# LayerNorm sums moved from GpSimd back to the tensor engine, and a narrower halo, in an eight-core macaron block

## What is computed

```python
x = x + 0.5 * ffn(layernorm(x), w1, b1, w2, b2)
x = x + attn(layernorm(x), ...)
x = x + 0.5 * ffn(layernorm(x), w1, b1, w2, b2)
```

## Time and profile before

| | us |
|---|---|
| median of the two runs shown | 5175.09 (5070.04 and 5280.14) |
| profiled execution | 5069.3 |
| its span, first to last instruction, slowest core (7) | 5067.8 |
| spans of the eight cores | 5056.0 to 5067.8 |
| TensorE matmul busy | 4774.9 (94%) |
| VectorE, ScalarE, GpSimd busy | 512.8, 402.2, 289.6 |
| granted TensorE clock, mean over the span, eight cores | 0.970 to 0.974 |

### The profile page before, as it was taken

One profiled execution on the slowest core, in us unless ns is written; L12 is line 12 of the kernel. 1 busy time (PEld: TensorE's weight loads), 2 busy tenths in 40 slices (PEclk: granted clock), 3 DMA queues, 4 the chain that ended last, 5 costly groups with the idle time before them and its releaser, 6 DMA issues.

```text
span 5067.8 us, 31354 instructions; the slowest of 8 cores (5056.0 to 5067.8 us)
## 1 busy us (share of the span) xinstructions
PE 4774.9 (94%) x11994; PEld 2274.3 (45%) x11994; DVE 512.8 (10%) x721; ACT 402.2 (8%) x628; POOL 289.6 (6%) x360
## 2 busy tenths in 40 slices
PE   5999999999999996999979798599999999999999
PEld 2555555555555552444534333244444444444444
DVE  1010010010010002223223311101000100000000
ACT  1101101101100101111000000100011001100100
POOL 2000000000000001111000000200010010000000
PEclk9999999999999997999989999799999999999999
DMA  4222222222222221333321101022222222222222
GB/s 121 92 85 90 92 87 88 91 87 92 87 89 90 90 89 42 113 105 105 122 87 32 59 27 29 25 75 79 86 72 75 80 89 67 77 85 83 75 84 77
DMA packets 116244, 408.04 MB, mean 81 GB/s; under 512 B 13825, under 2 KB 20097, under 8 KB 116097
## 3 DMA queue, kind: packets, MB, share of 16 engines
q1 hardware_dynamic: 103298, 362.43, 22.5%
q0 software_dynamic: 12800, 43.61, 2.5%
HBM read 379.73 MB, written 26.25 MB: 80 GB/s over the span
## 4 chain that ended last, share of the span: by engine, by line
PE 92%; DVE 2%; DMA 2%; POOLq 1%; issue 1%; ACT 1%; POOL 0%; ACTq 0%; SPq 0%; DVEq 0%
PE ps L150 92%; POOLq L190 1%; DVE pool L165 1%; DMA pool<-gate_sc 1%; ACT pool L160 1%; POOL pool L191 0%; DVE pool L325 0%; DMA pool<-win_cat 0%; DMA X<-T_fm 0%; DVE pool L181 0%; DVE pool L334 0%; DMA pool<-wout_cat 0%; SPq L185 0%; ACTq L54 0%; DVEq L54 0%
## 5 line engine op out<-in xcount | busy, mean ns | idle before, releaser
L150 PE MATMUL ps<-pool 128*128 128x436 f32 (+2 forms) x11792 | 4672.7, 559 | 167.5 <-DVE pool L165 51.5
L150 PEld LDWEIGHTS ps<-pool 128*128 128x128 f32 x11792 | 2249.2, 192 | 2594.3 <-issue 2593.7
L160 ACT ACTIVATE pool<-ps,smalls_s 128x436 f32<-128x436 f32 (+1 forms) x328 | 212.8, 649 | 1782.0 <-PE ps L150 1781.7
L181 DVE SCALAR_TENSOR_TENSOR X<-pool,smalls_s,X 128x436 f32<-128x436 f32 (+1 forms) x72 | 51.0, 708 | 2068.3 <-ACT pool L160 2068.3
L160 ACT ACTIVATE pool<-ps 128x436 f32<-128x436 f32 (+3 forms) x105 | 58.3, 555 | 1776.1 <-PE ps L150 1767.2
L165 DVE TENSOR_TENSOR pool<-pool 1x436 f32<-1x436 f32 (+1 forms) x24 | 17.7, 737 | 1563.2 <-ACT pool L160 1562.7
L160 ACT ACTIVATE pool<-X 128x436 f32<-128x436 f32 (+1 forms) x112 | 65.5, 585 | 895.5 <-DVE X L181 420.1
L150 PE MATMUL ps<-pool,ones_c 128*1 128x436 f32 (+1 forms) x126 | 56.7, 575 | 66.0 <-POOL pool L191 64.4
L185 POOL DMA_DIRECT2D out_fm<-X x32 | 17.3, 542 | 1748.6 <-DVE X L181 1748.6
L150 PE MATMUL ps<-pool,ones_r 1*128 1x436 f32 (+1 forms) x76 | 48.3, 771 | 53.1 <-DVE pool L165 27.3
L191 POOL TENSOR_TENSOR pool<-X 128x436 f32<-128x436 f32 (+1 forms) x14 | 16.0, 1146 | 1418.7 <-DVE X L181 744.9
(11 more groups left out here) (26 smaller groups left out, 272.9 us busy)
## 6 DMA issues: line engine op xcount, KB each, us to landing
pool<-w1r SPq DMA_DIRECT2D x288, 512.0 KB, 3.3
pool<-w2r SPq DMA_DIRECT2D x288, 512.0 KB, 3.3
pool<-in_wr SPq DMA_DIRECT2D x80, 512.0 KB, 3.5
X<-T_fm SPq DMA_DIRECT2D x5, 1744.0 KB, 22.1
x_sc<-pool POOLq DMA_DIRECT2D x40, 218.0 KB, 2.9
gate_sc<-pool POOLq DMA_DIRECT2D x40, 218.0 KB, 3.1
pool<-gate_sc POOLq DMA_DIRECT2D x32, 256.0 KB, 3.0
out_fm<-X POOLq DMA_DIRECT2D x32, 256.0 KB, 2.3
```

The lines of the kernel that those rows point to most:

```text
L150: e.matmul(o, l, r, start=s, stop=p), inc=inc)
L160: e.activation(out=o, in_=i, func=f, **k), inc=inc)
L181: e.scalar_tensor_tensor(out=o, in0=a0, scalar=s_, in1=a1, op0=p0, op1=p1),
```

## The change

Two things. The sums of LayerNorm no longer use GpSimd: `stats_pre`, its buffers and `gtt` are gone, and `stats` does 8 matmuls against the column of ones straight from `X` for the sum, then 8 for the squares, each fed by a ScalarE square through two buffers. In the projection stage `stats`, `rows` and `bcast` move from after groups 4, 5, 6 to after groups 0, 1, 2. And the halo shrinks from 66 to 51 columns on each side, so that NT is 2150 and the five tiles are 430 columns wide. (The offsets of the buffers in SBUF follow from the new width; the output weights of the scan stage lie elsewhere.)

```diff
-NT = 2180
-C0, C1 = 66, 2114
+W_WIN = 50
+NT = 2048 + 2 * (W_WIN + 1)
+C0, C1 = W_WIN + 1, W_WIN + 1 + 2048
...
-            def stats_pre(self, ts_, te_, in_sem=None, xg=0):
...
-                gtt(x8, xv(0, ts_, te_), xv(1, ts_, te_), ALU.add, inc="G")
-                for k in range(2, DC):
-                    gtt(x8, x8, xv(k, ts_, te_), ALU.add, inc="G")
...
-            def stats(self, ps_free_v=0):
+            def stats(self, ts_, te_, ps_free_v=0, in_sem=None):
...
-                mm(p_sum[0:1, :w], ONESC[:, :], x8, True, True,
-                   inc=None if self.sq_g else "T")
-                if self.sq_g:
-                    mm(p_sq[0:1, :w], ONESC[:, :], sqa, True, True, inc="T")
...
+                for k in range(DC):
+                    mm(p_sum[0:1, :w], ONESC[:, :], xv(k, ts_, te_), k == 0, k == DC - 1,
+                       inc="T" if k == DC - 1 else None)
+                for k in range(DC):
+                    par = k % 2
+                    b.wait("scalar", "T", self.sq_tmarks.get(par, 0))
+                    act(pv(self.sq + par * 512, w), xv(k, ts_, te_), AF.Square, inc="S")
+                    b.wait("tensor", "S")
+                    mm(p_sq[0:1, :w], ONESC[:, :], pv(self.sq + par * 512, w), k == 0,
+                       k == DC - 1, inc="T")
+                    self.sq_tmarks[par] = b.cnt["T"]
...
-                        if m == 4:
-                            lnp2.stats()
-                        elif m == 5:
+                        if m == 0:
+                            lnp2.stats(FT[ti + 1][0], FT[ti + 1][1])
+                        elif m == 1:
                             lnp2.rows()
-                        elif m == 6:
+                        elif m == 2:
                             lnp2.bcast(tn_marks[ti])
```

More of the change, by code:

```diff
@@ L8 @@
 ALU = mybir.AluOpType
-NT = 2180
-C0, C1 = 66, 2114
+W_WIN = 50
+NT = 2048 + 2 * (W_WIN + 1)
+C0, C1 = W_WIN + 1, W_WIN + 1 + 2048
 D, DC = 1024, 8
 H, HC = 4096, 32
-FT = [(i * 436, (i + 1) * 436) for i in range(5)]
+FTW = NT // 5
+assert FTW * 5 == NT and FTW % 2 == 0 and FTW <= 512
+FT = [(i * FTW, (i + 1) * FTW) for i in range(5)]
 BT = [(C0 + i * 512, C0 + (i + 1) * 512) for i in range(4)]
-PW = [(1, 437), (437, 873), (873, 1309), (1309, 1745), (1745, 2179)]
+PW = [(1 + i * FTW, min(1 + (i + 1) * FTW, NT - 1)) for i in range(5)]
 POOL_W = 35000
 MASKBC = 0
[L20 to L29, removed]
+DATA1 = NT
+ABARBC = 2 * NT
+HS = 3 * NT
+YS = 4 * NT
+P1_LNX = 0
+P1_HT = P1_LNX + 2 * 8 * FTW
+P1_WB1 = P1_HT + 32 * FTW
+P1_WB2 = P1_WB1 + 2048
+P1_SQ = P1_WB2 + 2048
+P1_BT = P1_SQ + 1024
+P1_RW = P1_BT + 1024
+P2_TN = NT
+P2_WBI = P2_TN + 8 * NT
+P2_SQ2 = P2_WBI + 2048
+P2_TMP = P2_SQ2 + 1024
+P2_SCR = P2_TMP + 1024
+P2_RW = P2_SCR + 1024
+P2_MROW = P2_RW + 3584
+P3_PWW = HS
+P3_WIN = P3_PWW + 8192
+P3_XS = P3_WIN + 1024
+P3_XC = P3_XS + 4 * (FTW + 4)
+P3_XP = P3_XC + 4 * (FTW + 4)
+P5_YG = YS + 2048 + 64
+P5_GT = P5_YG + 4096
+P5_OW = P5_GT + 1024 + 64
+P5_WOC = 33792
+P5_TMP = P5_OW
 P6_LNX, P6_HT, P6_WB1, P6_WB2, P6_SQ, P6_BT, P6_RW = 0, 8192, 24576, 26624, 28672, 29696, 30720
-P6_TR = 33792
 SB1, SB2, SINB, SPWB, SOUTB, SDW, SDWB, SNS = 0, 32, 40, 56, 64, 72, 96, 104
@@ new lines, in stats @@
+                b.wait("tensor", "G", g_ones)
+                if in_sem is not None:
+                    b.wait("tensor", in_sem, 16)
+                    b.wait("scalar", in_sem, 16)
+                for k in range(DC):
[9 more added lines that the diff above has]
+                    self.sq_tmarks[par] = b.cnt["T"]
@@ L498, in build_nc @@
                 mask_smark = b.cnt["S"]
-            lnp2 = LNPipe(P2_RW, P2_SQ2, "ln2", banks=(ps2, ps3, ps4, ps6, ps7), tr=P2_TR, sq_g=False)
+            lnp2 = LNPipe(P2_RW, P2_SQ2, "ln2", banks=(ps2, ps3, ps4, ps6, ps7))
             ts0, te0 = FT[0]
-            lnp2.stats_pre(ts0, te0)
-            lnp2.stats()
+            lnp2.stats(ts0, te0)
             lnp2.rows()
@@ L510, in chain_emit @@
                 w = te_ - ts_
-                b.wait("vector", "G", lnp2.pre_gmark)
-                b.wait("vector", "S", lnp2.sq_smark_done)
                 b.wait("vector", "T", lnp2.bcast_tmark)
@@ L735, in build_nc @@
             b.wait("vector", "V", p5_tile_vmark[3])
-            ln3 = LNPipe(P6_RW, P6_SQ, "ln", banks=(ps6, ps7, ps5, ps4, None), tr=P6_TR)
+            ln3 = LNPipe(P6_RW, P6_SQ, "ln", banks=(ps6, ps7, ps5, ps4, None))
             ffn3 = Ffn(P6_LNX, 4096, P6_HT, P6_WB1, P6_WB2, P6_BT, ln3)
```

88 lines of the change are left out of this document (13 added, 75 removed).

## The result

| | before | after |
|---|---|---|
| median of all executions, us | 5248.78 (10, 5070.04 to 5922.5) | 5525.07 (11, 5155.18 to 6109.65) |
| ratio, 95% interval | | 1.0202 (1.0147 to 1.0256) |
| profiled execution, its span | 5069.3, 5067.8 | 5123.53, 5122.0 |
| median span of undisturbed cores | 5063.6 (30) | 5089.7 (46) |

A forecast was written before the change was run, and what follows sets the result against it. TensorE, busy 94% of the span, was taken as the bound; terms from -36.5 (width) to +43.6 (first-FFN sums) came to +17.7 us on the span of 5067.8, giving 5087 us, +0.35%, with a range of 5066 to 5193.

The forecast's parts named there:

- Sums between the products: Blocks of sums between the FFNs' products: 10.9 us more each in the first (+43.6), 12.6 in the second (+37.8).
- what was said of the clock: TensorE at 1.2 GHz after idle stretches, 2.4 in long ones; the skill's 13/16 rule not seen in the trace.
- width: Tiles 6 columns narrower shorten TensorE's matmuls, sums and broadcasts throughout: -36.5 us together.
- a block, first FFN; second: Length of 8 matmuls from X plus 8 on squares between products: 12.5 us first FFN, 14.4 second.
- its start, a part of that: TensorE's sums no longer wait for GpSimd at an FFN's start: -6.8 us first FFN, -18.7 second.
- projection stage: Seven more matmuls at four boundaries, +20.2 us, and +4.7 at the stage's start, partly at half clock.
- wait of 1.89 us: Projection stage: TensorE's wait for the broadcast's rows stays, because two groups still lie between.
- The first: Rival at FFN starts and second-FFN stalls: waits for GpSimd stay, -6.8, -18.7, -26.6 lost, time 5139 us; chance 0.06.
- The fourth: Rival on the sums: one-column matmuls overlap neighbours and cost half, time 5025 us, -0.9%; chance 0.06.
- The second: Rival at 14 sums blocks: gaps between squares' matmuls lower the clock, 158 us, time 5245; chance 0.03.
- The third: Rival on whole stretches: less clock because TensorE no longer pauses, 210 us more, time 5297; chance 0.03.

The follow-up runs named there:

- the last kernel: Kernel before with halo 51, full-width ones, GpSimd's sums kept, `stats_pre` of tile i+2 moved behind tile i+1's normalization: lowest 5026.43 us, ratio 0.9861.

## Why the prediction was wrong

The time was forecast as no change and came out at +2.0% (1.5 to 2.6). **The step that failed** is in "Sums between the products" and in what was said of the clock: the blocks were priced by their instructions alone, 10.9 and 12.6 us each, and the products behind them at full clock. The runs show a price behind the block, 30 us for a stretch at 0.81, on one pair of cores or another and not behind every block; added to the kernel before, such blocks cost 4.4% with one column and 1.6% at full width, with the same instructions. The metric takes the slowest core, so it takes nearly every time the worst pair. In the profiled execution the slowest core had one; in the four other executions of the result in which no whole die was longer, the slowest pair lay 64 to 95 us above the undisturbed cores, which would be two or three. (Only profiled executions show the stretches themselves; for the others this is worked out from the spans.)

By its terms, from undisturbed cores (stage bounds of before from its core 5, after from its core 3):

| term or stage | forecast | measured |
|---|---|---|
| width | -36.5 | -40 (halo alone) |
| a block, first FFN; second | 12.5; 14.4 | 12.47; 14.45 |
| first FFN in all | +10.9 | +7.8 |
| its start, a part of that | -6.8 | -11.7 (on core 7 -12.5) |
| projection stage | +17.6 | +23.3 |
| convolution and scans | -3.6 | -3.5 |
| second FFN to its last matmul | -7.5 | -6.3 |
| its start, a part of that | -18.7 | -18.6 |
| behind the last matmul | 0 | +7 |
| stages together | +17.4 | +28.4 |
| clock behind the blocks | 0 | about three quarters of the 2%: 1.020 with the column, 1.003 at full width |

The last sum is that of two cores; over all undisturbed cores it is +26. (The forecast's terms, put together by stage, give 17.4, 0.3 off their sum by rounding.) The start of the first FFN gained more, because TensorE begins at 11.46 (core 7) and not at the 16.7 that the forecast took from GpSimd's start. The projection stage lost 5.7 us more. The earlier trace rows show its first boundary, and there the wait of 1.89 us did not stay, and the broadcast behind it runs at half clock. Core 3 after, timeline, answers to the earlier trace rows; the last line is core 5 before, at its fourth boundary:

```profile
2051.96 11.82 PE L170 MATMUL ps<-pool 128*128 128x430 f32 x32
2066.16 4.63 PE L170 MATMUL ps<-pool,ones_r 1*128 1x430 f32 x6 [2.38 <-DVE pool L185]
...
2404.77 4.69 PE L150 MATMUL ps<-pool,ones_r 1*128 1x436 f32 x6 [3.62 <-DVE pool L165]
```

6 instructions take 4.63 us for 2.43 before. But that boundary was the only one of the four at which the kernel before had a short wait: at the others its waits were 3.17, 3.17 and 3.62 us and the broadcast took 4.12 to 4.69 already. Over the four, the waits come to 12.5 us for 11.9 and the broadcasts to 18.5 for 15.8, which is 3.3 of the 5.7; the rest is not assigned. So the forecast's "wait of 1.89 us" was not that of the stage. The two groups that cover the chain of row operations are themselves shorter (11.82 for 11.97 us), so the narrower tiles give part of their gain back in the waits. The last 7 us stand behind the last matmul: the end of the span comes 13.5 us after it, before 6.4. All the kernels without arithmetic on GpSimd in which I looked have it (the changed one, the sums alone, full-width ones), the ones with it do not; why was not tried.

**The rivals.** The first, that the waits for GpSimd do not go, fell. The fourth, half-price one-column matmuls, fell: 16 in 5.93 us. The second named the right place, the clock at the blocks, with the wrong mechanism: nothing falls within the block, whose length is as forecast, and its counter-evidence (1.00 around the projection's block) looked at a block of 7.5 us, and only at the 19 us around it on one core. The third had the right kind, less clock on whole stretches, and the wrong cause: it is not that TensorE no longer pauses, since the last kernel pauses less than before and is faster, and the kernel before with blocks pauses as ever and has the stretches. The second and the third together had a chance of 0.06.

The rule of the Trainium skill (TensorE: Matmul & The Clock Gate, Part 1) that the forecast set aside deserved more. It describes a limit on peak current at 13/16 of the clock. The level measured is 0.81, which is that. Its condition and extent do not agree with the profiles of these runs: the rule has three dense cores of a die set it off for the whole die as long as the load lasts, and here eight dense cores run at 1.00 most of the time, and pairs fall, mostly for 160 us, and come back under full load. That a step in current brings the kernel to the level would fit what the width of the block does, and was not measured. Because the rule was plainly not in force in the long products, I took its level as out of play, and did not ask what else might bring the kernel to it.

## What to carry to other kernels

A block of one-column matmuls of 12 us amid full products is not paid for with its own length alone: on an eight-core program look at the granted clock of every core for the 200 us behind it. If such sums have to be on TensorE, use ones as wide as the array; the instructions are no longer for it, and here that alone brought the changed kernel from 1.020 to 1.003 (in two series, each against the kernel before). And ask first whether a stall needs an engine relieved, or only one queue put in another order: the order gave some 30 us here, while the change, which relieved the engine, removed the same stalls and paid for it with more matmuls and a lower clock.

## What the runs showed of the hardware that I had not expected

- Stretches of granted 0.81 that mostly last about 160 us and end with TensorE full, on two neighbouring cores at once (0 and 1, 2 and 3, 4 and 5, 6 and 7), starting 4 to 35 us behind a one-column block, on one pair and not on another in the same execution. Some are longer, 280 to some 2050 us. The Trainium skill (Trainium Architecture — The Big Picture, The hierarchy) calls such pairs of cores with shared infrastructure an SEngine; that they share a limit of current is my reading and was not measured.
- Behind full-width blocks of the same length no stretch was seen in an FFN: none on the eight cores of the changed kernel and of the kernel before with such blocks, nor on cores 4 to 7 of the former in its second profile.
- A sum of two one-column instructions put singly between full matmuls costs 0.29 us beyond its own length.
- A wait of 1.89 us left the granted clock at 1.00 and 6 instructions in 2.43 us; waits of 2.38 to 3.66 us were followed, on the cores read here, by 3.49 to 4.69 us for the same 6, and behind the one of 2.38 us the granted clock is 0.50.
- Open: what sets off the stretches in the projection stage, where full-width ones did not end them, and the two in the FFNs of a kernel without blocks of 16 sums; why some last longer; and the 7 us at the end.
